# Attention with relative positions on one core: products of values in one run per half step, relative products in two runs, a second buffer for the first weights

## The reference, cut to what matters

```
x: (8, 1024, 256)
xn = layernorm(x)
q, k, v = xn @ W.T + b                          # 16 heads of 16
rk, rv = embK[idx], embV[idx]                    # idx = clip(key - query, -64, 64) + 64
logits = q . k  +  q . rk[q, k]
w = softmax(logits)
out = w @ v  +  sum over k of w[q, k] * rv[q, k]
x = x + layernorm(out @ Wo.T + bo)
x = x + layernorm(layernorm(x) @ ternary(Wf).T * alpha + bf)
```

## Time and profile before

| | |
|---|---|
| median of three runs | 2827.56 us (2824.03 to 2828.02) |
| the profiled execution | 2825.32 us, span 2823.5 us |
| PE busy | 93% of the span |
| weight loads | 70% |
| DVE busy | 72% |
| ACT busy | 55% |
| POOL busy | 34% |
| chain that ended last | PE 69%, DVE 16%, issue 5%, ACT 4% |

### The profile page before, as it was taken

How to read it: one execution, slowest core, us unless ns; L and a number is a source line. 1 busy time by engine, 2 the same in 40 slices (tenths; PEclk the granted TensorE clock), 3 DMA queues, 4 the chain that set the end, 5 groups by cost and what they waited for, 6 DMA issues and landing times.

```text
span 2823.5 us, 102954 instructions
## 1 busy us (share of the span) xinstructions
PE 2627.9 (93%) x43410; PEld 1977.3 (70%) x43410; DVE 2035.1 (72%) x5187; ACT 1558.8 (55%) x2993; POOL 955.3 (34%) x2275
## 2 busy tenths in 40 slices
PE   5899999999999999999999999999999999999995
PEld 4577777677776777767776777767777677777773
DVE  4776678676786778866788667876678766787774
ACT  2455556455555555555555565545565455565651
POOL 3113333433334323343234332334323433331026
PEclk8799999999999999999999999999999999999997
DMA  7556654456454564555645556446654456445410
GB/s 220 173 136 177 174 150 125 128 153 186 123 152 131 160 166 135 134 149 156 172 119 147 164 153 168 118 124 176 167 143 126 115 174 187 137 131 144 133 44 27
DMA packets 605048, 409.11 MB, mean 145 GB/s; under 512 B 149162, under 2 KB 604330, under 8 KB 604330
## 3 DMA queue, kind: packets, MB, share of 16 engines
q1 hardware_dynamic: 604586, 402.54, 50.7%
HBM read 206.84 MB, written 194.90 MB: 142 GB/s over the span
## 4 chain that ended last, share of the span: by engine, by line
PE 69%; DVE 16%; issue 5%; ACT 4%; POOL 3%; SPq 2%; DMA 1%; DVEq 0%; ACTq 0%; POOLq 0%
PE oacc L797 15%; PE logitsT L759 15%; PE scores L736 14%; PE logitsT L764 7%; DVE maxes L1016 6%; DVE junk L1013 5%; PE misc L860 4%; PE misc L693 4%; PE misc L822 3%; PE misc L834 2%; PE misc L710 2%; PE misc L810 2%; ACT wxr L1216 2%; POOL rs L1249 1%; PE misc L720 1%
## 5 line engine op out<-in xcount | busy, mean ns | idle before, releaser
L1013 DVE CUSTOM_DVE_ANT_1 junk<-scores,bands 128x512 bf16<-128x512 f32 x988 | 679.7, 688 | 594.4 <-PE scores L736 575.4
L759 PE MATMUL logitsT<-qs,ks 98*128 98x128 bf16 (+3 forms) x9088 | 995.2, 216 | 32.2 <-ACT wxr L1216 23.3
L1216 ACT ACTIVATE wxr<-logitsT 128x512 f32<-128x512 f32 x1024 | 601.9, 602 | 568.2 <-PE logitsT L759 471.4
L759 PEld LDWEIGHTS logitsT<-qs,ks 98*128 98x128 bf16 (+1 forms) x9088 | 679.6, 99 | 256.5 <-issue 95.9
L1216 ACT ACTIVATE wy<-logitsT 128x512 f32<-128x512 f32 x1024 | 587.2, 597 | 437.6 <-PE logitsT L759 427.0
L736 PE MATMUL scores<-ks,qs 101*128 101x256 bf16 (+10 forms) x4096 | 719.1, 291 | 78.5 <-DVE maxes L1016 39.0
L1016 DVE TENSOR_REDUCE maxes<-scores 128x1 f32<-128x512 f32 x1024 | 701.5, 685 | 2.3 <-PE scores L736 2.3
L736 PEld LDWEIGHTS scores<-ks,qs 96*128 96x128 bf16 (+3 forms) x4096 | 299.0, 99 | 265.2 <-DVE maxes L1016 120.1
L764 PE MATMUL logitsT<-ident,bands 128*128 128x128 f32 x2048 | 468.0, 280 | 0.0
L1244 POOL TENSOR_SCALAR rs<-rs 128x1 int32<-128x1 int32 (+1 forms) x224 | 48.3, 216 | 995.5 <-DVE rs L924 992.9
L764 PEld LDWEIGHTS logitsT<-ident,bands 128*128 128x128 f32 x2048 | 292.5, 143 | 33.4 <-issue 0.6
(11 more groups left out here) (136 smaller groups left out, 2587.0 us busy)
## 6 DMA issues: line engine op xcount, KB each, us to landing
bs<-praw SPq DMA_DIRECT2D x256, 512.0 KB, 4.3
bands<-bs SPq DMA_DIRECT2D x224, 512.0 KB, 4.4
ks<-kd SPq DMA_DIRECT2D x64, 384.0 KB, 5.0
qs<-qd SPq DMA_DIRECT2D x112, 192.0 KB
bands<-bs SPq DMA_DIRECT2D x128, 128.0 KB, 3.8
qd<-qparts SPq DMA_DIRECT2D x64, 192.0 KB, 3.2
kd<-kparts SPq DMA_DIRECT2D x64, 192.0 KB, 2.6
qd<-qparts SPq DMA_DIRECT2D x64, 128.0 KB, 2.6
```

The source lines that it names most:

```text
L759: mm = e.matmul(lt[:, c * P + q0:c * P + q1], kk[0:depth, h, kt * P:(kt + 1) * P], qs[i][0:depth, h, q0:q1], start=q0 == 0, stop=not near, ...
L1013: e.tensor_tensor_reduce(junk[:], scores[:, 0:512].rearrange("p (a c) -> p a c", a=2), banded, 1.0, LOWEST, ALU.add, ALU.max, mx[:, h, 0:1 ...
L1216: e.activation(dst, src, ACT.Exp).then_inc(exp_ready, 1)
```

## The change

The X products of a half step move from slot o + 2.4 to o + 4.09, just before the Y products at o + 4.1, so that all eight key tiles are one run; the merge moves from o + 3.5 to o + 4.9. The last half step of each quad (`alone`) keeps the old slots. `wr` gets space for eight heads, so `wxr` grows from 36 to 40 pieces of 256 columns, and an exponential of X in the second half step no longer waits for the X products of the first; it waits for those of the same half of the step before. The four pieces of each relative part become one run of 64 instructions at the first piece's slot, and the bank plan loses what it had for pieces.

```diff
-            at(o + 2.4, "weighted", s, blk, "X")
+            alone = i == QUAD - 1 and blk
+            at(o + (2.4 if alone else 4.09), "weighted", s, blk, "X")
             at(o + 4.1, "weighted", s, blk, "Y")
-            at(o + 3.5, "merge", s, blk)
+            at(o + (3.5 if alone else 4.9), "merge", s, blk)
...
-                for piece in range(4):
-                    at(z + 29.6 + 1.5 * part + 0.35 * piece, "relative", quad, part, piece)
+                at(z + 29.6 + 1.5 * part, "relative", quad, part)
...
         if stage in HOLD:
-            bank = held if stage == "relative" and k[2] else until.index(min(until))
-            if stage == "relative" and k[2]:
-                slot += kept
-            else:
-                late, slot = max(0, until[bank] - slot), max(slot, until[bank])
-            if stage == "relative":
-                held, kept = bank, late if k[2] == 0 else kept
-            until[bank] = slot + (10 if stage == "relative" and k[2] < 3 else HOLD[stage])
+            bank = until.index(min(until))
+            slot = max(slot, until[bank])
+            until[bank] = slot + HOLD[stage]
...
-        wxr = sb("wxr", [P, (QUAD * HG + 4) * WIN])
+        wxr = sb("wxr", [P, (QUAD + 1) * HG * WIN])
...
-        wr = wxr[:, QUAD * HG * WIN:].rearrange("p (j c) -> p j c", j=4)
+        wr = wxr[:, QUAD * HG * WIN:].rearrange("p (h c) -> p h c", h=HG)
...
-                                    src = wr[:, j, (c - 2) * P + q0:(c - 2) * P + q1]
+                                    src = wr[:, h, (c - 2) * P + q0:(c - 2) * P + q1]
...
-                    quad, part, piece = k
+                    quad, part = k
...
-                    for i in range(8 * part + 2 * piece, 8 * part + 2 * piece + 2):
+                    for i in range(8 * part, 8 * part + 8):
...
-                    if piece == 3:
-                        mm.then_inc(rel_summed, 1)
+                    mm.then_inc(rel_summed, 1)
...
-                    if h >= 4:
-                        act.wait_ge(done, value["pv" + kind, s, 0])
+                    if kind == "X":
+                        if s:
+                            act.wait_ge(done, value["pvX", s - 1, h // 4])
+                    elif h >= 4:
+                        act.wait_ge(done, value["pvY", s, 0])
                     elif s:
-                        act.wait_ge(done, value["pv" + kind, s - 1, 1])
+                        act.wait_ge(done, value["pvY", s - 1, 1])
```

More of the change, by code:

```diff
@@ L192, in with_banks @@
     timed, until = [], [-1000.0 - i for i in range(NMISC)]
-    held = kept = 0
     for slot, stage, k in sorted(slots, key=lambda x: x[0]):
@@ L269, in counts @@
             for stage, k in orders[engine]:
-                if stage in stages and not (stage == "relative" and k[2] < 3):
+                if stage in stages:
                     n += 1
@@ L287, in misc_banks @@
             continue
[L288 to L294, removed]
+        plan[(stage,) + k] = (bank,) + free[bank]
+        signal = FREED_BY[stage]
+        free[bank] = (signal, 1 if stage == "ternary" else value[(signal, stage) + k])
     return plan
@@ L1042, in vector_program @@
                                                ALU.mult).then_inc(merged, 1)
-                elif stage == "relative" and k[2] == 3:
-                    quad, part, _ = k
+                elif stage == "relative":
+                    quad, part = k
                     dve.wait_ge(rel_summed, 2 * quad + part + 1)
@@ L1207, in scalar_program @@
                         at_ = (s % QUAD * HG + h) * WIN
-                        dst = bass.AP(wxr, at_, [[(QUAD * HG + 4) * WIN, P], [(QUAD * HG + h % 4) * WIN - at_, 2], [1, WIN]])
+                        dst = bass.AP(wxr, at_, [[(QUAD + 1) * HG * WIN, P], [(QUAD * HG + h) * WIN - at_, 2], [1, WIN]])
                         src = lt[:].rearrange("p (a c) -> p a c", a=2)
```

## The result

The changed kernel takes 2969.18 us (median of four runs, 2967.57 to 2974.24), the kernel before 2827.79 in the same series: ratio 1.0507, 95% interval 1.0491 to 1.0522. The sign and the mechanism of the forecast (2905) held, the size didn't: the loss is 141 us and not 78. The time lies 19 us above the forecast's own range (2840 to 2950) and 4 us above the wide one (2768 to 2965). The profiled execution is the slowest of the four: 2974.24 us, span 2972.4, so its trace is 149 us longer than the one before and not 141.

A forecast was written before the change was run, and what follows sets the result against it. PE and DVE were taken to wait for each other at a score buffer holding one head. The profiled 2825.3 us + 86 (net waits less switches) - 5 (second buffer) = 2906, forecast 2905 us, range 2840 to 2950.

The forecast's parts named there:

- the wide one: The range of total time given for 8 in 10: 2768 to 2965 us.
- PE's 93% hides waits: At the score buffer: 174 us of PE's weight loads already wait for a reduction to free its half.
- the merged run: X and Y products of values back to back, 64 instructions: 1.00 + 1.00 - 0.12 = 1.88 us.
- the working of the sample: One half step traced through: the merge delays the next head's reduction, PE waits, 1.15 us longer instead of 0.21 shorter.
- Net +2.85 us per four steps: Half steps +3.25 and relative products -0.4; over 30 x four steps, +86 us.
- The relative products: One run of 64 instructions per part, 1.3 us, no more than DVE has in store: -0.4 us per four steps.
- The half steps: Costs of moving runs and merge, per four steps: 1.15 + 0.7 + 0.6 + 0.6 + 0.2 = 3.25 us.
- the switches: Entering and leaving column-tiled runs of values on PE: 224 saved at 0.21 us each, 47 us.
- Rival C: DVE takes over: merges, output normalisation and tails collide after each long run, 5 us or more per four steps; 2970 us; chance 0.12.
- A (the switches decide): On PE: added waits are absorbed and saved switches make it faster, 2765 to 2790 us; chance 0.27.
- The summed time of L797: Sign at the line of the products of values: its summed time falls by about 20 us in either case.
- right behind most L1038: Sign at the merge: a wait of the scores' weight loads (L736) for DVE stands right behind most merges.

The follow-up runs named there:

- the twins with light work of DVE: The kernel before and the changed kernel, both with the two reductions and the merge on fewer columns: 2697.3 and 2725.2 us.
- rel_two: The kernel before with only the relative products of each part in one run of 64 instructions: 2833.5 us, ratio 1.0025.
- the late merge: The changed kernel with the merge at slot o + 7.0 for steps 0 to 2 of a quad: 2918.9 us, ratio 1.0335 to the kernel before.
- closed_runs: The changed kernel with the Y products at o + 4.091, so nothing sorts between them and the X products: 2959.2 us, ratio 1.0456 to the kernel before.

## Why the prediction was right in kind and wrong in size

**Right.** PE's busy share falling (93% to 90%) while the span grows. The reading that PE's 93% hides waits; that the run's old place filled an interval in which DVE works and its new one doesn't; 1.88 us for the merged run (1.87); the working of the sample up to the wait for DVE (3.94 us against 3.86); the second buffer at nothing (1.0000); weight loads of L726 at 308 us, far over 174; fewer and longer waits of DVE.

**The step that failed is the sum over the half steps**: "Net +2.85 us per four steps". Measured are 141 / 30 = 4.7. Every term of it is a wait or a switch; the clock, which gave the largest part of what was missed, has no term. From the starts of the scores in both traces (mean of the 26 quads from the fourth on; the time from the first scores of a step to those of the next step; in the last column the 12 of these quads that have no more time at the lower clock than before):

| scores of | stand beside the weights of | before | after | difference | prediction | difference, clock as before |
|---|---|---|---|---|---|---|
| step 2 | step 0 | 20.38 | 22.63 | +2.25 | 1.15 + 0.2 | +1.55 |
| step 3 | steps 1, 2 (first half) | 26.36 | 26.90 | +0.54 | 0.7 + 0.2 + 0.2 | +0.16 |
| step 0 of the next | steps 2 (second half), 3 | 18.96 | 20.30 | +1.34 | 0.6 + 0.2 | +1.23 |
| step 1 of the next | step 3, relative | 19.25 | 19.52 | +0.27 | 0 - 0.4 | +0.32 |
| sum | | | | +4.40 | +2.85 | +3.27 |

Three terms were mis-sized, the largest first.
1. The clock, put at nothing without a reason. Of the 1.55 us missed per quad (4.40 - 2.85) it is 0.9 by the line (4.40 - 3.52) and 1.1 by the last column (4.40 - 3.27); over the whole kernel an estimated 30 to 40 us. In the sample it made four tail products 0.8 us longer. Without it the kernel would be near 2935 us, inside the forecast's own range. That the twins with light work of DVE have nearly the same clock (0.982 and 0.981) shows that it came with the waits.
2. The relative products, -0.4 predicted. rel_two measured +7 us, 0.2 per quad, so "no more than DVE has in store" was wrong. The waits for the first reduction rose with it (53.6 to 80.6 us); which work of DVE they stand behind isn't shown.
3. The half steps, each by itself. With the clock as before, the scores of step 2 came out 0.2 us above the forecast, those of step 0 0.4 above and those of step 3 0.9 below; these nearly cancel. Beside step 2's scores DVE has the output's normalisation and a tail step to do in the sample. Why step 0's came out higher and step 3's lower isn't shown.

Beside these, the switches saved were 162, not 224, 13 us less gain by the 0.21.

**How the cases stood.** Rival C named the mechanism (merges, normalisation and tails collide after each long run) and the number, and had 0.12. The number is partly luck: C has 5 us of waits per four steps, and the waits are 3.3 to 3.5, nearer to the forecast's 2.85; the clock makes the rest. The sample worked through was a fair one for the steps behind a quad's end: 1.15 + 0.2 predicted there, 1.55 measured with the clock as before. A (the switches decide) is out: 34 us of switches stand against 141 + 34 = 175 of new waits and clock. Two signs failed. The summed time of L797 did not fall by 20 us but rose from 554 to 566: from 200 us on, a product's record is marked 0.41 us long while the clock is low and 0.26 us otherwise. And a wait does not stand "right behind most L1038": within 2 us of the end of a merge, the weight load of some scores waited 0.2 us or more for a reduction at 94 of 224 merges (32 before).

The Trainium skill's page TensorEngine Tiling (Array Packing), PSUM Bottleneck, says that tiling speeds up TensorE and not the evacuation of PSUM, which may become the bottleneck. No run here tests that: the products that PE waits to write, scores and logits, are not tiled. What the trace adds is that a bottleneck need not be one of sums: the engines that empty PSUM are 72% and 55% busy, and yet 135 of the 141 us go when their work is made light in both kernels.

## What to carry to other kernels

Before two runs of small products are joined to save a switch (here 0.21 us), look at what each hides: a run standing between two products that wait for the same one-deep buffer is free cover, and beside an interval that is long already it hides nothing more. Do the sum for every interval between two fillings of that buffer, with everything the other engine does in it, not for one place and then by analogy. And when slots decide the order, check that what is to be adjacent can't tie with anything: 0.01 slot wasn't enough.

## What the runs showed of the hardware

- A lower clock came with waits: the mean granted clock fell from 0.981 to 0.968 with additional waits of up to 1.6 us in a PE that is marked 90% busy. It was 0.975 with 0.22 us of repeated matmuls at 224 places, and 0.980 with the late merge. A microsecond at the lower level costs 0.40 us here, by the line through 26 quads.
- Additional PE work at a place where PE waits is nearly free: 50 us of repeated matmuls made the kernel no slower, and a quad with the same clock 0.16 us longer for 1.5 us of work.
- Joining column-tiled runs saves 0.21 us per switch by the starts, and 0.16 by closed_runs, or 0.10 if 4 of its 10 us are clock.
